# A sparse transformer block on one core: the large block's third tile behind two down products, two gather buffers of its own, a block table computed in four places

## The reference

```python
x = x + cross(layernorm(x), ids, ctx, ctx, ctx)     # silu(h W^T) * (h W^T) W, one of 4 experts by id
h = rmsnorm(layernorm(x)) * norm_w
scores = softmax(h @ gate_w.T); w, ids = top_k(scores, 4); w = w / sum(w)
routed[t] = sum_k w[t, k] * ((silu(h[t] @ Wg[e]) * (h[t] @ Wu[e])) @ Wd[e]),  e = ids[t, k]
shared = (silu(h @ shared_gate) * (h @ shared_up)) @ shared_down
out = x + layernorm(x) + routed + shared
```

## Time and profile before

| | us |
|---|---|
| three runs | 659.65, 659.98, 662.21 |
| median | 659.98 |
| the profiled execution: its own time | 663.33 |
| the profiled execution: its span | 661.4 |
| PE busy | 598.8 (91%) |
| DVE busy | 442.4 (67%) |
| ACT busy | 361.0 (55%) |
| POOL busy | 360.4 (54%) |

### The profile page before, as it was taken

One profiled execution on the slowest core, in us unless ns is written; L12 is line 12 of the kernel. 1 busy time (PEld: TensorE's weight loads), 2 busy tenths in 40 slices (PEclk: granted clock), 3 DMA queues, 4 the chain that ended last, 5 costly groups with the idle time before them and its releaser, 6 DMA issues.

```text
span 661.4 us, 13810 instructions
## 1 busy us (share of the span) xinstructions
PE 598.8 (91%) x3665; PEld 516.4 (78%) x3667; DVE 442.4 (67%) x1033; ACT 361.0 (55%) x603; POOL 360.4 (54%) x369
## 2 busy tenths in 40 slices
PE   2899999999998999799999999999999999999990
PEld 1777788888786877689879888888987978888870
DVE  6778888876997795575666657566565665756620
ACT  5547666665321224456566566665756666666540
POOL 5736777556320113536656566575665755666432
PEclk9999999999997999799999999999999999999995
DMA  7511233447642585868898988989898898888453
GB/s 290 185 40 59 94 111 135 169 163 240 210 51 31 116 222 100 263 177 225 220 270 207 243 231 229 261 196 275 204 231 258 213 254 214 236 251 198 104 61 51
DMA packets 43469, 120.50 MB, mean 182 GB/s; under 512 B 5808, under 2 KB 6960, under 8 KB 42928
## 3 DMA queue, kind: packets, MB, share of 16 engines
q0 software_dynamic: 22720, 55.06, 39.0%
q1 hardware_dynamic: 20720, 65.09, 29.0%
HBM read 88.42 MB, written 36.96 MB: 190 GB/s over the span
## 4 chain that ended last, share of the span: by engine, by line
PE 27%; issue 16%; DVE 13%; ACT 9%; DVEq 5%; DMA 4%; POOL 1%; ACTq 1%; POOLq 0%; SPq 0%
ACT wh L1239 5%; DVE wl L1395 4%; PE sps_t L210 3%; PE sps_gu L210 3%; PE sps_t L212 3%; PE sps_gu L212 3%; PE sps_gu L211 3%; PE sps_t L211 3%; DVEq L177 3%; ACT s_xth L1245 2%; DVE s_xtl L1401 2%; DVE both L1574 2%; PE sps_table L1142 1%; PE sps_cols L1136 1%; PE sps_y L210 1%
## 5 line engine op out<-in xcount | busy, mean ns | idle before, releaser
L1395 DVE TENSOR_TENSOR wl<-raw,wh 128x1024 fp32r<-128x1024 f32 x96 | 116.4, 1223 | 65.5 <-ACT wh L1239 50.9
L1239 ACT ACTIVATE wh<-raw 128x1024 fp32r<-128x1024 f32 x96 | 100.9, 1051 | 1.1 <-DMA raw<-in_experts_w 1.1
L1008 POOL DMA_INDIRECT both<-hb_dram,gather x64 | 78.3, 1223 | 32.3 <-issue 18.6
L1020 POOL DMA_INDIRECT out<-r_oh,scatter x32 | 51.1, 1598 | 69.5 <-ACT r_oh L1303 57.7
L210 PE MATMUL sps_gu<-s_xth,wh 128*128 128x256 f32 (+1 forms) x256 | 78.3, 306 | 2.2 <-DVE s_xtl L1401 1.1
L211 PE MATMUL sps_gu<-s_xtl,wh 128*128 128x256 f32 (+1 forms) x256 | 76.6, 299 | 0.0
L212 PE MATMUL sps_gu<-s_xth,wl 128*128 128x256 f32 (+1 forms) x256 | 76.6, 299 | 0.0
L210 PEld LDWEIGHTS sps_gu<-s_xth,wh 128*128 128x128 f32 x256 | 49.3, 193 | 9.4 <-issue 8.0
L1020 POOL DMA_INDIRECT out<-r_rank,scatter x16 | 25.9, 1616 | 51.2 <-DMA out<-spare_tiles,scatter 29.3
L211 PEld LDWEIGHTS sps_gu<-s_xtl,wh 128*128 128x128 f32 x256 | 49.3, 193 | 0.6
L212 PEld LDWEIGHTS sps_gu<-s_xth,wl 128*128 128x128 f32 x256 | 49.3, 193 | 0.0
(11 more groups left out here) (389 smaller groups left out, 1804.2 us busy)
## 6 DMA issues: line engine op xcount, KB each, us to landing
raw<-in_experts_w SPq DMA_DIRECT2D x96, 512.0 KB
craw<-in_ctx_w SPq DMA_DIRECT2D x4, 1024.0 KB, 7.9
out<-hb_dram SPq DMA_DIRECT2D x4, 1024.0 KB, 13.3
out<-both POOLq DMA_DIRECT2D x13, 256.0 KB, 4.1
both<-hb_dram SPq DMA_DIRECT2D x10, 256.0 KB, 5.3
spare_tiles<-hb_dram SPq DMA_DIRECT2D x6, 256.0 KB, 6.1
both<-hb_dram,gather POOLq DMA_INDIRECT x64
sraw<-in_sg SPq DMA_DIRECT2D x1, 512.0 KB
```

What stands on the lines that cost most here:

```text
L1008: pool.indirect_dma_start(e_xg[j][0:n], None, hn_rows, bass.IndirectOffsetOnAxis(ap=gidx[0:n, j:j + 1], axis=0)).then_inc(e_gx[j], 16)
L1020: pool.indirect_dma_start(m.out, bass.IndirectOffsetOnAxis(ap=sidx[0:n, j:j + 1], axis=0), e_y[j][0:n], None, compute_op=ALU.add).then_inc ...
L1239: nc.scalar.activation(m.wh[:, b, ROWS[part]], m.raw[:, b, ROWS[part]], ACT.Copy).then_inc(e_hi[b][part], 1)
L1395: dve.tensor_tensor(m.wl[:, b, ROWS[part]], m.raw[:, b, ROWS[part]], m.wh[:, b, ROWS[part]].bitcast(F32), ALU.subtract).then_inc(e_lo[b][p ...
```

## The change

- TensorE's round: down 3 of the round before moves ahead of tile 4's transposes; ScalarE and VectorE take the rows of tiles 2 and 3 ahead of the second half of the small block's activations, and the next rows of tiles 0 and 1 ahead of the second half of the large block's.
- The gather buffers of tiles 2 and 3 move from `both` to two free tiles of `late`. Their first gathers don't wait for the shared stage's scatters any more; the waits stand behind them.
- The block table is computed in four pieces, at i = 3, 4, 5 and 6, and `TABLED` is 9.
- In the last round the small block's down products, scalings and scatter indices stand before the large block's gate-up.

```diff
-        TABLED = 7
+        TABLED = 9
...
-        e_xg = [xg[:, 0], xg[:, 1], xg[:, 2], xg[:, 3], late[:, 0:D]]
+        e_xg = [xg[:, 0], xg[:, 1], late[:, 4 * D:5 * D], late[:, 5 * D:6 * D], late[:, 0:D]]
...
                 if i == LATE:
-                    pool.wait_ge(sums[0], 16 * ((G - 3 + 1) // 2))
-                    gather(2, 0)
-                    pool.wait_ge(sums[1], 16 * ((G - 3) // 2))
-                    gather(3, 0)
-                    pool.wait_ge(s["g1"], LATE)
-                    gather(4, 0)
+                    for j in TILES[1]:
+                        gather(j, 0)
+                    for q in range(2):
+                        pool.wait_ge(sums[q], 16 * ((G - 3 + 1 - q) // 2))
...
                 turned_rows(3, turn)
                 if not first:
                     down(2, turn - 1)
+                    down(3, turn - 1)
                 turned_rows(4, turn)
                 if not first:
-                    down(3, turn - 1)
                     down(4, turn - 1)
+                if last:
+                    down(0, turn)
+                    down(1, turn)
                 gate_up(1, turn)
                 if not last:
                     turned_rows(0, turn + 1)
                     turned_rows(1, turn + 1)
-                down(0, turn)
-                down(1, turn)
+                    down(0, turn)
+                    down(1, turn)
...
                 high_a(0, 0, turn)
-                high_a(0, 1, turn)
                 high_rows(2, turn)
                 high_rows(3, turn)
+                high_a(0, 1, turn)
...
+                if last:
+                    columns = columns_of(act, m.tab2, 0, turn)
+                    scaled(0, columns[0], turn)
+                    scaled(1, columns[1], turn)
                 if not last:
                     weights(0, "rows_a", turn + 1)
                 silu(1, 0, turn)
...
                 high_a(1, 0, turn)
-                high_a(1, 1, turn)
                 if not last:
                     high_rows(0, turn + 1)
                     high_rows(1, turn + 1)
-                columns = columns_of(act, m.tab2, 0, turn)
-                scaled(0, columns[0], turn)
-                scaled(1, columns[1], turn)
+                high_a(1, 1, turn)
+                if not last:
+                    columns = columns_of(act, m.tab2, 0, turn)
+                    scaled(0, columns[0], turn)
+                    scaled(1, columns[1], turn)
...
-                if i == TABLED - 3:
+                if i == 3:
                     dve.tensor_scalar(is_small, m.part_id[:], float(MAX_TURNS), None, ALU.is_lt)
...
+                if i == 4:
                     dve.tensor_scalar(n_half, upto[:, E2 - 1:E2], 0.5, 0.25, ALU.mult, ALU.add)
...
+                if i == 5:
                     k_(dve.tensor_tensor(inside, nth, length, ALU.add))
...
+                if i == 6:
                     dve.tensor_copy(cols[:, 0:1], found[:, 0:1])
...
                 gated(0, 1, turn)
-                low_half(0, 1, turn)
                 low_rows(2, turn)
                 low_rows(3, turn)
+                low_half(0, 1, turn)
+                if last:
+                    add_rows(0, turn)
                 low_rows(4, turn)
                 if not last:
                     gather_rows(1, turn + 1)
                     low_weights(0, "rows_a", turn + 1)
                     low_weights(0, "rows_b", turn + 1)
-                add_rows(0, turn)
+                    add_rows(0, turn)
                 low_weights(1, "rows_c", turn)
+                if last:
+                    add_rows(1, turn)
                 gated(1, 0, turn)
                 low_half(1, 0, turn)
                 gated(1, 1, turn)
-                low_half(1, 1, turn)
                 if not last:
                     low_rows(0, turn + 1)
                     low_rows(1, turn + 1)
+                low_half(1, 1, turn)
...
             step(turns - 1, last=True)
-            add_rows(1, turns - 1)
```

More of the change, by code:

```diff
@@ L1472, in _ @@
             k_(dve.tensor_copy(sel[:, 2], seli[:, 2]))
+            two_tiles, whole, large, length, upto, ahead, begin, seg, nth, inside = (blk[:, r] for r in (0, 0, 1, 2, 3, 4, 5, 5, 6, 7))
+            value = blk[:, 8:11]
+            n_half, n_whole, n_turns, is_small, slot, place_of = (blkcol[:, r:r + 1] for r in range(6))
+            found = blkcol[:, 5:8]
+            many = blk[:, 7]
+            n_large = ahead[:, E2 - 1:E2]
             for i in range(2, TILED + 1):
@@ L1480, in _ @@
                     low_weights(0, early(i), 0)
-                if i == TABLED - 3:
-                    two_tiles, whole, large, length, upto, ahead, begin, seg, nth, inside = (blk[:, r] for r in (0, 0, 1, 2, 3, 4, 5, 5, 6, 7))
-                    value = blk[:, 8:11]
-                    n_half, n_whole, n_turns, is_small, slot, place_of = (blkcol[:, r:r + 1] for r in range(6))
-                    found = blkcol[:, 5:8]
-                    many = blk[:, 7]
+                if i == 3:
                     dve.tensor_scalar(is_small, m.part_id[:], float(MAX_TURNS), None, ALU.is_lt)
@@ L1496, in _ @@
                     k_(dve.tensor_tensor_scan(upto, length, row[:, 3, :], 0.0, ALU.add, ALU.add))
-                    n_large = ahead[:, E2 - 1:E2]
+                if i == 4:
                     dve.tensor_scalar(n_half, upto[:, E2 - 1:E2], 0.5, 0.25, ALU.mult, ALU.add)
```

## The result

The changed kernel takes 643.77 us (median of 4 runs, 639.49 to 644.82) against 660.44 for the kernel before (median of 4 beside it): ratio 0.9732, 95% interval 0.9682 to 0.9781. It is faster, as forecast, by 16.7 us and not by 22.5: inside the stated range of 631.5 to 647, but just above the 632 to 643 of the forecast itself. The profiled execution took 644.35 us and has a span of 642.4.

A forecast was written before the change was run, and what follows sets the result against it. TensorE was taken to bound the rounds, but for one 1.46 us hole each. Terms -20.9 + 5.3 - 3.2 - 3.7 = -22.5 us gave 637.5 us on the median; range 631.5 to 647, the forecast's own 632 to 643.

The forecast's parts named there:

- rival (a): Middle rounds: they stop at the scatter chain or the DMA engines, about 22.7 us each; total 646.5; chance 0.12.
- Edit 1: Middle rounds, down product 3 before tile 4's transposes, rows before second activations: rounds of 22.05 us for 23.54, 20.9 us won.
- It fits, barely: POOL's scatter chain per round: 21.7 us needed with two landings of 8.0, against a round of 22.05.
- the rival's second ground: DMA engines in the rounds: share 0.89 before, 0.95 for the same work in 22.05 us.
- Edits 2 and 3: Shared stage: table in four places wins 4.7 us, TABLED at 9 costs 7.7 of stall and 2.3 of clock; 5.3 slower.
- The even step of the copies: Shared stage, sign that the forecast is right: copies of y at an even step through tiles 3 to 8.
- Edit 4: Join, own gather buffers for tiles 2 and 3: large gate-up at 271.0 instead of 273.80; 3.2 us won, bounds 0 to 5.1.
- rival (e): Join: the clock holds, as the two holes get shorter than 2.75 us; 1.9 us less, total 635.6; chance 0.12.
- Edit 5: Last round, small block's down products before the large gate-up: 3.7 us won, bounds 6.1 and -1.8.
- the rows of add 2 come ... say 1.6 us later than now: Last round: add 2's rows ready at 643.3, its scatter going at 644.1 without waiting for a landing.
- by 637: Last round: add 4 of round 14 has landed by then, so adds 0 and 1 can go.
- The sum: Whole kernel: -20.9 + 5.3 - 3.2 - 3.7 = -22.5 us, profiled span 661.4 to 638.9; on the median 637.5.

The follow-up runs named there:

- Two outputs: Changed kernel with the large block's three scatters sent to a second tensor and no scatter waiting for the other block's landing: 639.51 us.
- 8 instead of 9: Changed kernel with its block table read at iteration 8, not 9: 634.13 us, ratio 0.9592 to the kernel before.
- the order alone: Kernel before with only the middle rounds' new order on the three engines: 638.61 us, ratio 0.9686.
- the last round alone: Kernel before with only the new order of the last round: 660.54 us, ratio 0.9999.
- half the weight bytes: Changed kernel whose middle-round loads of routed weights bring one of two row groups (output wrong by that): 640.73 us.
- 7, 8 and 9: Iteration at which the changed kernel reads its block table: 640.20 us at 7, 634.13 at 8, 643.77 and 641.67 at 9.

## Why the prediction was right and where its steps failed

The direction came as forecast, and so did what edits 1 to 4 do where they act. The size did not: 643.77 is inside the range because the range took in rival (a), the chain of scatters, and it is rival (a) that happened, in a milder form. It lies nearer to that rival's 646.5 than to the forecast's 637.5. Part of the agreement is luck: in the profiled execution the clock held in the join, which is worth 1.5 us; when the same kernel ran again it fell, and the rounds happened to lose less.

- **Edit 1, -20.9 (measured -15.1; alone -21.2).** The step that priced the order is right: intervals of 21.98 for a forecast of 22.05, no idle at tile 4's rows, no wait in their place. The step that failed is "It fits, barely". It took both landings at 8.0 us and called that the longest seen. The trace of before has longer ones, up to 8.54 (add 1 to add 2 of round 5):

```profile
407.38 1.83 POOL L1020 DMA_INDIRECT out<-spare_tiles,scatter  x1 [0.30 <-issue]
...
415.92 1.62 POOL L1020 DMA_INDIRECT out<-r_rank,scatter  x1 [3.08 <-DMA out<-spare_tiles,scatter]
```

  With one such the sum is 5.7 + 8.5 + 8.0 = 22.2, over 22.05 already, and the second landing, that of add 4, could not be read there, as add 0 waited for its scaled copy. In the changed kernel both were 8.7 to 8.8 at the first slip, and one reached 9.7 once the chain was late. Rival (a) had the mechanism and was mis-sized: it wanted all rounds at 22.7, and the loss comes only after the chain has lost its slack. Two outputs shows the chain as the cause, and that the DMA share, the rival's second ground, is none.
- **Edits 2 and 3, +5.3 (measured +5.0).** The main terms came as forecast: 11.71 us of ScalarE's wait (I had 11.7 as the bound), 7.5 of TensorE's (7.7), half clock behind it; from the copy of y 3 to that of y 7 it takes 24.40 us where it took 28.96, 4.6 won for 4.7. The even step of the copies that I wanted as a sign isn't there (4.9, 6.9, 4.9 and 7.8 us). Not foreseen was that 8 instead of 9 turns +5 into a gain of 4.
- **Edit 4, -3.2 (measured -5.1, with the clock up; -3.6 when the changed kernel ran again).** The starts were priced right: tile 4's transposes and the large gate-up come at 272.06 and 273.48, which is 269.5 and 270.9 on the time axis of before, for 269.6 and 271.0. Both the forecast and rival (e) occurred in the same program. In totals it was worth 1 to 3 us on the changed kernel and nothing on the order alone; the later rounds' lag is where it may have gone, which is argued and not shown.
- **Edit 5, -3.7 (measured -1.4).** The order alone has the same tail (43.84), so the 1.2 to 1.4 us belong to edit 1, which takes its hole out of round 15 too. The failed step is "the rows of add 2 come ... say 1.6 us later than now": they come 3.9 later (the scaled copy ends 25.3 us into the round before, 29.2 after). I had the holes at 1.0 and 2.0 us, they are 1.00 and 2.87, and I had no term for the clock, which stands at 0.50 from 624.09 to 626.09, behind the second hole (in the last round alone it stands at 1.00 behind one as long). A second step, "by 637" for the landing of add 4 of round 14, fails with a lagging chain: add 0 goes at 22.1 us into the round for a forecast of 20.6. Either is enough alone: with half the weight bytes adds 0 and 1 go at 19.9 and 21.8, and add 2 still at 30.2, 1.0 behind its copy.
- **The sum**, -22.5 (measured -19.0, of which 2.4 lie ahead of all that is changed, so -16.6): 5.8 us were missing in the rounds and 2.3 in the tail, 1.9 more than forecast came in the join and 0.3 in the shared stage.

## What to carry to other kernels

When a hole is taken out of a loop, add up the loop's other chains at their longest landing in the whole trace, not at that of one round: with 0.35 us of slack in 22.05 by the prediction's own sum (1.6%), this chain of accumulating DMAs that must see each other's landings fell behind and stayed behind. A landing measured at one place of the round says little of the same landing 2 us later in it. A value that starts a far-off transfer can be read too early as well as too late, so its neighbours are worth trying: 7, 8 and 9 gave 640, 634 and 642 to 644 us. Try each part of a bundle alone; here one of four alone (638.6) gave no less than the whole.

## What was not expected of the hardware

- With the same two holes in the join (1.14 or 1.15 us, then 0.98) the granted clock held in two profiles (joins of 20.17 and 20.13 us) and fell to 0.50 in seven (21.5 to 21.7). The windows of the changed kernel's second profile, where the first has 1.00:

```profile
272.00:274.00 2.00, 0.92 (x6) 0.84 (x7) 1.47 (x4) 1.33 (x2) 0.00 (x0) 0.86 1.02 379
274.00:276.00 2.00, 2.00 (x9) 2.00 (x8) 1.48 (x4) 0.00 (x0) 1.15 (x1) 0.50 1.02 418
```

  TensorE never stood for more than 1.15 us at a time there, so the clock can fall without a longer stand, and need not; it cost 1.5 us. The Trainium skill (TensorE: Matmul & The Clock Gate, What's actually happening) lets the clock go by how busy TensorE has been, and names an idle stretch as the condition of the lower level; these rows agree with the first and show both outcomes for the same holes. What decides between them is not shown.
- An accumulating scatter of 128 rows of 2 KB needed 5.9 to 6.3 us from its start to that of the next one that waits for its landing where no weights are loaded (rounds 14 and 15), and up to 9.7 (10.5 in the run with the order alone) in rounds in which the DMA engines move 236 to 243 GB/s in all.
